# Second expert choices added to the token's own row, scatters one after another, in a perceiver block

## The reference, cut to what matters

```
def _L0_ffn_ref(x, gate_w, w1, w2, w3):
    xf = x.reshape(B * S, D)
    logits = xf @ gate_w
    scores = jax.nn.softmax(logits, axis=-1)
    top_scores, top_idx = jax.lax.top_k(scores, TOP_K)
    scale = jnp.zeros((T, E), dtype=x.dtype).at[jnp.arange(T)[:, None], top_idx].set(top_scores)
    xs = scale.T[:, :, None] * xf[None, :, :]
    h = jax.nn.silu(jnp.einsum('etd,edh->eth', xs, w1)) * jnp.einsum('etd,edh->eth', xs, w3)
    y = jnp.einsum('eth,ehd->etd', h, w2)
    out = y.sum(axis=0)
x = x + _L0_ffn_ref(_layernorm(x, axis=-1), ...)
```

## Time and profile before

| | us |
| --- | --- |
| median of 3 runs | 691.26 (690.44 to 692.63) |
| the profiled execution, its own time | 692.71 |
| its span | 691.0 |
| PE busy | 665.9 (96% of the span) |
| POOL busy | 317.3 (46%) |
| granted TensorE clock, mean of the span | 0.994 |

### The profile page before, as it was taken

How to read it: one execution, slowest core, us unless ns; L and a number is a source line. 1 busy time by engine, 2 the same in 40 slices (tenths; PEclk the granted TensorE clock), 3 DMA queues, 4 the chain that set the end, 5 groups by cost and what they waited for, 6 DMA issues and landing times.

```text
span 691.0 us, 13793 instructions
## 1 busy us (share of the span) xinstructions
PE 665.9 (96%) x4699; PEld 553.6 (80%) x4699; DVE 442.5 (64%) x778; ACT 418.5 (61%) x808; POOL 317.3 (46%) x278
## 2 busy tenths in 40 slices
PE   5999999999999999999999999999999889999996
PEld 3677888889888888888888878887888768888874
DVE  7785667465774666646766378864677747555573
ACT  3755776675775757757477554665655545656650
POOL 1554554551455415544255348528700044555525
PEclk9999999999999999999999999999999899999999
DMA  9995354345533454425522263511072557665648
GB/s 258 194 164 146 107 152 125 90 112 133 149 107 76 123 152 124 119 61 152 152 91 73 81 192 114 198 61 42 20 246 106 197 171 173 115 103 112 111 94 328
DMA packets 95063, 91.97 MB, mean 133 GB/s; under 512 B 11441, under 2 KB 68785, under 8 KB 95025
## 3 DMA queue, kind: packets, MB, share of 16 engines
q1 hardware_dynamic: 89728, 79.14, 41.4%
q0 software_dynamic: 4720, 11.27, 8.8%
q10 hardware_dynamic: 576, 1.05, 0.4%
HBM read 71.52 MB, written 19.92 MB: 132 GB/s over the span
## 4 chain that ended last, share of the span: by engine, by line
PE 88%; DMA 5%; DVE 3%; issue 1%; ACT 1%; SPq 1%; POOL 0%; DVEq 0%; ACTq 0%; POOLq 0%
PE pK L34 48%; PE pVP L34 21%; PE pVP L1801 5%; PE pTU L1839 2%; PE pTU L1858 2%; DMA fin<-total 2%; PE pTU L1689 1%; PE pTU L2040 1%; DMA big<-x_rows,idx_x 1%; PE pVP L1942 1%; PE pVP L1848 1%; PE pS L1848 1%; DMA bn_vec<-in_L_attn_vq_dram 1%; PE pS L1970 1%; DMA total<-big,idx 1%
## 5 line engine op out<-in xcount | busy, mean ns | idle before, releaser
L34 PE MATMUL pK<-parts 128*128 128x512 f32 (+1 forms) x768 | 178.4, 388 | 0.0
L34 PEld LDWEIGHTS pK<-parts 128*128 128x128 f32 x768 | 138.7, 188 | 33.4 <-issue 5.8
L602 POOL TENSOR_TENSOR parts<-ctxR,parts 128x1024 fp32r<-128x1024 f32 x28 | 66.9, 2408 | 148.4 <-ACT parts L841 148.4
L34 PE MATMUL pVP<-pT,parts 128*128 128x256 f32 x768 | 95.7, 283 | 1.3 <-ACT z L878 0.9
L34 PEld LDWEIGHTS pVP<-pT,parts 128*128 128x128 f32 x768 | 92.3, 189 | 2.9 <-issue 2.3
L586 POOL TENSOR_TENSOR parts<-big,parts 128x1024 fp32r<-128x1024 f32 x32 | 76.9, 2424 | 3.3 <-ACT parts L757 3.3
L34 PE MATMUL pK<-w,lhs 128*128 x276 | 69.1, 399 | 0.7 <-issue 0.2
L1294 DVE TENSOR_SCALAR z<-pVP 128x512 f32<-128x512 f32 x32 | 22.1, 691 | 62.7 <-PE pVP L34 62.7
L34 PEld LDWEIGHTS pK<-w,lhs 128*128 128x128 f32 x276 | 50.2, 188 | 11.5 <-issue 1.8
L857 ACT ACTIVATE prob<-prob,neg_max 128x257 f32<-128x257 f32 x64 | 32.1, 504 | 36.1 <-DVE neg_max L1260 36.1
L1629 DVE TENSOR_TENSOR w_p<-big,w_p 128x1024 fp32r<-128x1024 f32 x22 | 27.0, 1225 | 37.9 <-ACT w_p L1080 37.9
(11 more groups left out here) (319 smaller groups left out, 1424.6 us busy)
## 6 DMA issues: line engine op xcount, KB each, us to landing
big<-in_ctx_dram SPq DMA_DIRECT2D x32, 512.0 KB, 4.2
big<-in_ctx_dram SPq DMA_DIRECT2D x120, 128.0 KB, 2.9
total<-zero SPq DMA_DIRECT2D x32, 256.0 KB, 4.4
w_raw<-in_L_ffn_w_dram SPq DMA_DIRECT2D x16, 512.0 KB, 6.2
big<-in_L_ffn_w_dram SPq DMA_DIRECT2D x8, 512.0 KB, 6.3
fin<-total SPq DMA_DIRECT2D x8, 512.0 KB, 8.5
total<-big SPq DMA_DIRECT2D x8, 256.0 KB, 2.4
x_rows<-big SPq DMA_DIRECT2D x8, 256.0 KB, 2.0
```

The lines of the kernel that those rows point to most:

```text
L34: last = pe.matmul(out, lhs(a, c), rhs(b, c), start=start and c == first and n == 0, stop=stop and c == chunks - 1 and n == 2)
L602: nc.gpsimd.tensor_tensor(ctxT[:, :, LO, part], ctxR[:, :, part], ctxT[:, :, HI, part].bitcast(F32), ALU.subtract).then_inc(ctx_lo, 1)
```

## The change

Both choices of a token are added to row 4T + n. To keep two additions to one row from overlapping, `scatter(j)` first waits until `scatter(j - 1)` has landed. The final loads bring one block (256 KB for each group of 128 tokens) where they brought two, and the seven additions on POOL and the one on DVE that joined the blocks go. The zeroing of `total` is unchanged.

```
-        fin = at("fin", [P, TOP_K, TILES, D], 0)
+        fin = at("fin", [P, TILES, D], 0)
...
             for t in range(TILES):
-                sp.dma_start(fin[:, :, t, :], chosen_t[:, :, t, :]).then_inc(fin_in[t][0], 16)
+                sp.dma_start(fin[:, t, :], total_t[:, t, :]).then_inc(fin_in[t][0], 16)
...
-            nc.gpsimd.iota(block_of[:, :, :], [[-T, TOP_K], [P, TILES]], base=4 * T, channel_multiplier=0, allow_small_or_imprecise_dtypes=True)
+            nc.gpsimd.iota(block_of[:, :, :], [[0, TOP_K], [P, TILES]], base=4 * T, channel_multiplier=0, allow_small_or_imprecise_dtypes=True)
...
             def scatter(j):
                 pool.wait_ge(y_set, j + 1)
+                if j >= 1:
+                    pool.wait_ge(added[(j - 1) % 2], 16 * ((j + 1) // 2))
                 nc.gpsimd.indirect_dma_start(total[:, :], bass.IndirectOffsetOnAxis(idx[:, j:j + 1], 0),
...
-            for t in range(TILES - 1):
-                pool.wait_ge(*fin_in[t])
-                nc.gpsimd.tensor_tensor(fin[:, 0, t], fin[:, 0, t], fin[:, 1, t], ALU.add).then_inc(fin_sum, 1)
...
             for t in range(TILES):
-                if t == TILES - 2:
-                    dve.wait_ge(*fin_in[TILES - 1])
-                    tt(fin[:, 0, TILES - 1], fin[:, 0, TILES - 1], fin[:, 1, TILES - 1], ALU.add).then_inc(tok_set, 1)
-                if t < TILES - 1:
-                    dve.wait_ge(fin_sum, t + 1)
-                else:
-                    dve.wait_ge(tok_set, 2 + LAST + 1)
+                dve.wait_ge(*fin_in[t])
                 dve.wait_ge(fin_mm, t + 1)
-                tt(fin[:, 0, t], fin[:, 0, t], p_fin[t], ALU.add).then_inc(fin_add, 1)
+                tt(fin[:, t], fin[:, t], p_fin[t], ALU.add).then_inc(fin_add, 1)
```

More of the change, by code:

```diff
@@ L251, in perceiver_block @@
         total = nc.dram_tensor("total", (5 * T, D), F32, kind="Internal").ap()
-        chosen_t = total[3 * T:5 * T, :].rearrange("(k t p) d -> p k t d", k=TOP_K, p=P)
         blank = total[0:4 * T, :].rearrange("(t p) d -> p t d", p=P)
@@ L321, in perceiver_block @@
         fin_in = [(s, 64 + 16) for s in w13_in] + [(norm_in, 48), (rem_in, 112), (gate_in, 32), (bo_in, 32)]
-        fin_sum, fin_mm, fin_add, stored = (sem(n) for n in ("fin_sum", "fin_mm", "fin_add", "stored"))
+        fin_mm, fin_add, stored = (sem(n) for n in ("fin_mm", "fin_add", "stored"))
         tok_set, y_lo = sem("tok_set"), sem("y_lo")
@@ L522, in _ @@
             for t in range(TILES):
-                sp.dma_start(fin[:, :, t, :], chosen_t[:, :, t, :]).then_inc(fin_in[t][0], 16)
+                sp.dma_start(fin[:, t, :], total_t[:, t, :]).then_inc(fin_in[t][0], 16)
             for t in range(0, TILES, 2):
                 sp.wait_ge(fin_add, t + 1)
-                sp.dma_start(out_t[:, t, :], fin[:, 0, t, :]).then_inc(stored, 16)
+                sp.dma_start(out_t[:, t, :], fin[:, t, :]).then_inc(stored, 16)
             sp.wait_ge(stored, 16 * TILES)
@@ L1112, in _ @@
                 act.wait_ge(fin_add, t + 1)
-                act.dma_start(out_t[:, t, :], fin[:, 0, t, :]).then_inc(stored, 16)
+                act.dma_start(out_t[:, t, :], fin[:, t, :]).then_inc(stored, 16)
         @block.vector
```

## The result

| | before | changed |
| --- | --- | --- |
| median, us | 691.94 (4 runs, 690.44 to 694.97) | 704.89 (4 runs, 703.26 to 705.88) |
| span of the profiled execution | 691.0 | 703.8 |

The changed kernel is slower: the ratio is 1.0189, with a 95% interval of 1.0168 to 1.0211. Forecast were 699.4 us and a range from 694.0 to 703.7; the way was right, the loss of 13 us is over half as large again as the 8.2 forecast, and the median lies 1.2 us outside the range.

What follows compares the result with a forecast made beforehand. PE paces the slot loop; the added wait makes serial scatters (5.56 us against 4.85) the slowest thing. Loop +9.5 us and shorter end -1.3 give +8.2: 700.9 us profiled, 699.4 on the median, range 694.0 to 703.7.

Steps and rivals of the forecast that it cites:

- The chain of scatters: In the slot loop, serial scatters 5.56 us apart exceed the earlier 4.85 and bind from scatter 1 on.
- ACT's wait for `y_sb`: ACT's copy waits for the scatter two back; claimed to cost nothing while gathers hold PE back, 0.8 us later.
- The clock stays at 1.00: PE's granted clock in the slot loop was claimed to stay at 1.00 despite PE's stops.
- The end: After the loop, half the final load bytes and fewer additions were claimed to gain 1.3 us.
- Gather 22: Last gather: starts 1.90 us after scatter 16, lands after 4.2, lets PE go on at 669.24 instead of 659.73.
- PE's stops of 0.7 us a slot: PE waits for gathers before its transposes (line 2032), from slot 8 or so on, 9.5 us in all.
- (a): Slot loop: wait hidden, period 5.05 us or less, kernel not slower, 690.0 us if hidden whole; chance 0.12.
- (c): Slot loop: gathers have more room, PE is stopped less, the scatters' own end counts, 696.3 us; chance 0.08.
- (d): PE's clock falls because PE stands still 0.7 us in 5.56; over 80 us more; chance 0.02.
- (b): Scatters to the same 2 MB collide, landing about 5.25 us, period 6.0, 706.5 us; chance 0.06.
- the period of the serial chain: Scatter to scatter in the loop: landing 4.8 plus release 0.76 gives 5.56 us, between 5.22 and 5.82.
- The rule that I weighed: Skill's price for a scatter's landing, 2.6 us for 256 KB, would hide the chain, 690.0 us; chance 0.01.

Runs made afterwards that it cites:

- gather_first: The changed kernel with each gather issued one place earlier on POOL, ahead of the scatter that waits: 704.09 us, ratio 1.0183 to the kernel before.
- one_block_only: The changed kernel without its added wait, second choices on their own rows and never read: 689.98 us, ratio 0.9981 to the kernel before.
- wait_only: The kernel before with the added wait alone, second choices on their own rows, final loads and additions kept: 710.07 us, ratio 1.0266.

## Why the prediction was wrong in size

**Right, by its own steps.** The chain of scatters becomes the slowest thing in the loop, from the first scatter on; POOL is released by landings 19 times of 20. PE waits for the gathers that stand behind the waiting scatters, and ACT's wait for `y_sb` doesn't show while the gathers hold PE, but lies so near that it takes over when they don't (`gather_first`). The clock stays at 1.00. The end gives back 1.3 us (`one_block_only`). Gather 22 started 1.89 us behind scatter 16 and landed after 4.2, as forecast, 0.04 us before PE's transposes. That this path gives the right start of slot 22 is in part luck: the chain that ended last goes through gather 20, which landed after 5.4 us and not 4.2, and both paths reach slot 22 at the same time. PE's stops of 0.7 us a slot, 9.5 in all, did not come in that form; they are 6.4 us in ten stops and the slower starts. Of the rivals, (a) would have needed a pitch of 5.05, (c) and (d) did not come. (b) had the nearer time (706.5), but its mechanism is ruled out by `wait_only`.

**Wrong: the period of the serial chain**, 5.90 us for the 5.56 of the forecast and beyond its upper bound of 5.82. Over 16 slots that is 5.4 us too little, in two terms of "landing 4.8 plus release 0.76".

The release measured 0.88, not 0.76: 2.0 of the 5.4 us. I read it from the last scatter of the earlier trace rows, the only one with no other DMA behind it in POOL's queue. The trace of the kernel before had more already. ACT's copy before scatter 16:

```profile
650.32 0.60 ACT L1094 ACTIVATE big<-pVP 128x512 f32<-128x512 f32 x1 [0.85 <-PE pVP L34]
```

The scatter starts at 651.74, 0.82 after the copy's end; before scatter 0 it was 0.89. The row that I took as typical was the exception. The other 0.06 us come with the release by a landing, which no row of the kernel before could show.

The landing measured 5.01 us in the mean of the 16, not 4.8: 3.4 of the 5.4 us. Four of them make up 2.9 (5.05, 5.72, 6.05 and 5.32). I used the median where a chain adds up every member, and a bound from 20 landings of one execution, none of which had been in a chain. In the kernel before, a late landing would have had PE's time to hide in; in a chain nothing takes it back.

**The balance.** The chain began 0.75 us earlier in this execution (573.38 for 574.13). Then +5.4 for the periods; +0.5 from slot 22 to the last addition, because the hidden products behind transposes that wait for a gather start 0.85 us after them instead of 0.35; -0.4 for the last store (3.8 us from the last addition to the end, 4.2 before), which I had taken at nothing. Together that is +4.7, and the span is 703.8 where the forecast made 691.0 + 8.2 = 699.2; the 0.1 left over is rounding.

**The rule that I weighed.** The Trainium skill's price in "DMA: Bandwidth & Descriptors", section "Anatomy of one DMA — SWDGE (gpsimd) path", 2.6 us for 256 KB as an estimate from its figures, is near what the plain scatter took here (2.8 us). The scatter that adds took 4.8. I had set the rule aside for the trace, rightly, but not asked what it lacked; it was the addition.

## What to carry to other kernels

Before adding a wait on the previous transfer, make the sum landing plus release and hold it against the pitch of the work that feeds it: here 4.79 us separated no loss at all (plain or half-sized scatters, with the same wait) from 13 us of loss. Take the release from an instruction that has the same neighbours in its queue, and the landing as a mean with its stragglers, since a serial chain adds up each of them. And read what stands behind the wait in the same queue: here the gathers, with 1.8 us of slack, brought a DMA's lateness to TensorE.

## What the runs showed of the hardware

- An indirect DMA of 128 rows of 2 KB that adds to DRAM took 4.8 us to land in the median, one that writes 2.8; GpSimd's own part was 1.59 and 1.03 us. With rows of 1 KB the adding one took 3.8, with the same 1.59.
- From the end of ACT's copy to the start of such a DMA it took 0.77 us where no other DMA stood behind it in GpSimd's queue, and 0.82 where one did (0.89 at the first); from a landing to the start 0.84 and 0.88.
- In seven profiles with serial adding scatters 18 of 140 landings took 5.2 us or more, in four without a chain none of 80. Six of the 18 have a fetch of instructions that begins 2.1 to 3.4 us into them, where no fetch begins without a chain; ten have a longer instruction on GpSimd. What makes them late is open.
- Where TensorE's weight load waited for a gather, the matmuls behind the transposes started 0.82 to 1.01 us after them, and 0.35 us in the steady part of the kernel before, both at a granted clock of 1.00.
- Adding to rows that both choices share took no longer than adding to separate ones: the pitch was 5.90, 5.86 and 5.82 us in three profiles with shared rows and 5.82 with separate ones.
